# A graph attention layer on one core: x in four buffers, statistics spread over the step, and the masks made by GpSimd

## What is computed

```python
h = relu(layernorm(x))
q, k, v = h @ Wq + bq, h @ Wk + bk, h @ Wv + bv          # 12 heads
scores = q @ k.T / sqrt(32) + beta * adj
scores = where(adj > 0, scores, -9e15)
out = x + softmax(scores) @ v
```

## Time and profile before

| | us |
|---|---|
| median of 3 runs | 1084.06 (1083.67 to 1090.45) |
| the profiled execution | 1083.19 |
| span of its instructions | 1081.4 |
| TensorE busy | 995.7 (92%) |
| VectorE busy | 927.1 (86%) |
| ScalarE busy | 901.2 (83%) |
| GpSimd busy | 661.5 (61%) |
| TensorE's mean granted clock | 0.984 |

### The profile page before, as it was taken

One profiled execution on the slowest core, in us unless ns is written; L12 is line 12 of the kernel. 1 busy time (PEld: TensorE's weight loads), 2 busy tenths in 40 slices (PEclk: granted clock), 3 DMA queues, 4 the chain that ended last, 5 costly groups with the idle time before them and its releaser, 6 DMA issues.

```text
span 1081.4 us, 33411 instructions
## 1 busy us (share of the span) xinstructions
PE 995.7 (92%) x10587; PEld 674.7 (62%) x10587; DVE 927.1 (86%) x4256; ACT 901.2 (83%) x2384; POOL 661.5 (61%) x908
## 2 busy tenths in 40 slices
PE   3879999999999999999999999989999999999996
PEld 1346666666666666666666666656666666666764
DVE  6468889988888888888888888878888998889897
ACT  4368888888888888888888888878988889888887
POOL 2846666566765566755566766556766657676531
PEclk9889999999999999999999999998999999999997
DMA  4695688877669976767986757785678787868741
GB/s 155 112 184 103 160 158 177 182 141 134 157 152 167 173 153 133 160 147 170 168 174 137 148 155 162 172 177 114 141 162 167 172 176 142 146 143 163 149 105 45
DMA packets 234336, 163.15 MB, mean 151 GB/s; under 512 B 109744, under 2 KB 234160, under 8 KB 234160
## 3 DMA queue, kind: packets, MB, share of 16 engines
q1 hardware_dynamic: 233632, 160.23, 71.1%
q10 hardware_dynamic: 528, 0.79, 0.2%
HBM read 35.91 MB, written 25.17 MB: 56 GB/s over the span
## 4 chain that ended last, share of the span: by engine, by line
issue 22%; ACT 21%; POOL 20%; PE 16%; DVE 15%; DMA 2%; SPq 1%; POOLq 1%; DVEq 0%; ACTq 0%
ACT probs L541 11%; PE ps_p L463 9%; POOL v L358 7%; DVE biased L669 6%; POOL v L356 4%; PE ps_t L483 4%; ACT hn L556 4%; DVE kT L652 3%; POOL on L364 3%; DVE pT L675 3%; ACT qT L570 3%; POOL rstd L334 3%; ACT pT L575 2%; PE ps_s L475 2%; DMA xs<-in_x 2%
## 5 line engine op out<-in xcount | busy, mean ns | idle before, releaser
L541 ACT ACTIVATE probs<-biased,neg_max 128x128 f32<-128x128 f32 x1536 | 490.1, 395 | 95.2 <-DVE neg_max L669 85.0
L669 DVE CUSTOM_DVE_ANT_0 biased<-ps_s,mask 128x128 f32<-128x128 f32 x1536 | 354.2, 286 | 98.6 <-PE ps_s L475 61.7
L463 PE MATMUL ps_p<-hT,w 128*128 128x512 f16 x1728 | 420.7, 384 | 6.5 <-DVE qT L652 3.5
L364 POOL TENSOR_TENSOR on<-on,xb 128x384 f32<-128x384 f32 x128 | 127.5, 996 | 308.0 <-DVE on L690 308.0
L483 PE MATMUL ps_t<-ident,probs 128*128 128x128 f32 x1536 | 248.0, 284 | 33.7 <-ACT probs L541 26.2
L463 PEld LDWEIGHTS ps_p<-hT,w 128*128 128x128 f16 x1728 | 170.6, 99 | 160.5 <-issue 11.6
L675 DVE TENSOR_TENSOR pT<-ps_t,pT 128x512 f16<-128x512 f32 x384 | 263.5, 686 | 8.1 <-ACT pT L575 8.1
L575 ACT ACTIVATE pT<-ps_t 128x512 f16<-128x512 f32 x384 | 223.2, 581 | 1.0 <-PE ps_t L483 1.0
L463 PE MATMUL ps_p<-w,hT 128*128 128x384 f16 x1152 | 207.6, 326 | 0.0
L483 PEld LDWEIGHTS ps_t<-ident,probs 128*128 128x128 f32 x1536 | 162.6, 142 | 42.5 <-ACT probs L541 42.4
L475 PEld LDWEIGHTS ps_s<-k_st,q_st 96*128 96x128 f16 x1536 | 115.9, 98 | 97.2 <-DVE neg_max L669 20.8
(11 more groups left out here) (65 smaller groups left out, 1024.8 us busy)
## 6 DMA issues: line engine op xcount, KB each, us to landing
q_st<-qT SPq DMA_DIRECT2D x288, 128.0 KB, 3.3
k_st<-kT SPq DMA_DIRECT2D x288, 128.0 KB, 5.5
out<-on SPq DMA_DIRECT2D x128, 192.0 KB, 3.4
xs<-in_x SPq DMA_DIRECT2D x31, 768.0 KB, 6.1
adjs<-in_adj SPq DMA_DIRECT2D x32, 256.0 KB, 6.9
hT<-h_parts SPq DMA_TRANSPOSE x62, 4.4
xs<-in_x ACTq DMA_DIRECT2D x1, 768.0 KB, 6.3
k_st<-in_L_gnn_Wq SPq DMA_DIRECT2D x1, 576.0 KB, 6.5
```

What stands on the lines that cost most here:

```text
L364: pool.tensor_tensor(on[:, j % 2, :], on[:, j % 2, :], xb[:, par, j, :], ALU.add).then_inc(added, 1)
L463: mm = pe.matmul(dst, stationary, moving, start=m == 0, stop=m == MMS - 1)
L541: act.activation(probs[:, odd, i, :], biased[:, odd, i, :], ACT.Exp, bias=neg_max[:, odd, i:i + 1], scale=-1.0).then_inc(exp_done, 1)
L669: dve.tensor_tensor_reduce(out=biased[:, odd, i, :], in0=ps_s[:, i * N:(i + 1) * N], in1=mask[:, gp, v // CH, :], scale=-1.0, scalar=3.0e3 ...
```

## The change

There are four parts.

1. x has four buffers. x(1) and x(2) are loaded before the first step, and x(s+3) at the head of step s, behind the store of row block 1 and ahead of the first q spread; it waits for the readers of x(s-1).
2. The statistics of group s+2 are taken in step s one graph to a slot, in slots 0, 1, 9 and 10; `mean_var` has two buffers.
3. On GpSimd `rstd_of(s + 2)` stands in step s behind `split_v(s, ., 2)`, ahead of `add_x(s - 1, ., 1)`; before it was `rstd_of(s + 1)`, second in step s. `split_v(s, ., 2)` comes ahead of that addition too.
4. The mask is made by GpSimd, in three passes over 128x512 (two with one tensor input, one with two), behind `add_bias(s, ., 3)` and ahead of `add_x(s - 1, ., 0)`. VectorE's two passes are gone.

```diff
+    XB = 4
-        xs = sb("xs", [P, 2, G, D], F32)
+        xs = sb("xs", [P, XB, G, D], F32)
+        weighted = sb("weighted", [P, G, N], F32)
-        mean_var = sb("mean_var", [P, G, 2], F32)
+        mean_var = sb("mean_var", [P, 2, G, 2], F32)
...
-            sp.dma_start(xs[:, 1], x_v[1]).then_inc(x_in[1], 16)
+            for s in range(1, XB - 1):
+                sp.dma_start(xs[:, s], x_v[s]).then_inc(x_in[s], 16)
...
                 if 2 <= s <= STEPS:
                     store(s - 2, 1)
+                ahead = s + XB - 1
+                if ahead < STEPS:
+                    wait(sp, xb_done, G * s)
+                    wait(sp, normed, G * s)
+                    sp.nop(nofuse=True)
+                    sp.dma_start(xs[:, ahead % XB], x_v[ahead]).then_inc(x_in[ahead % XB], 16)
                 if proj:
                     spread(s, par, "q", 0)
...
-                if 0 <= s <= STEPS - 3:
-                    sp.wait_ge(xb_done, G * (s + 1))
-                    sp.wait_ge(normed, G * (s + 1))
-                    sp.nop(nofuse=True)
-                    sp.dma_start(xs[:, par], x_v[s + 2]).then_inc(x_in[par], 16)
...
+            def mask_of(s, par):
+                pool.wait_ge(adj_in, 16 * (s + 1))
+                wait(pool, biased_done, HPC * SLOTS * (s - 1))
+                pool.nop(nofuse=True)
+                wait(pool, mask_done, s)
+                pool.tensor_scalar(mask[:, par], adjs[:], 0.0, MASKED, ALU.is_le, ALU.mult).then_inc(mask_parts, 1)
+                pool.tensor_scalar(weighted[:], adjs[:], beta_col[:, 0:1], None, ALU.mult).then_inc(mask_parts, 1)
+                pool.wait_ge(mask_parts, 2 * (s + 1))
+                pool.tensor_tensor(mask[:, par], mask[:, par], weighted[:], ALU.add).then_inc(mask_done, 1)
...
                 if 1 <= s <= STEPS:
                     split_v(s - 1, 1 - par, G - 1)
-                if s >= 1 and s <= STEPS - 2:
-                    rstd_of(s + 1)
...
                 if proj:
                     add_bias(s, par, 3)
+                    mask_of(s, par)
                 if attend:
                     add_x(s - 1, 1 - par, 0)
                 if proj:
                     split_v(s, par, 0)
                     split_v(s, par, 1)
+                    split_v(s, par, 2)
+                if s <= STEPS - 3:
+                    rstd_of(s + 2, par)
                 if attend:
                     add_x(s - 1, 1 - par, 1)
-                if proj:
-                    split_v(s, par, 2)
...
-            def mask_unlinked(s, par):
-            def mask_linked(s, par):
...
+            def stats_in(s, u):
+                if s == 0:
+                    if u in (2, 3):
+                        return [(1, 2 * (u - 2)), (1, 2 * (u - 2) + 1)]
+                    return [(2, 2 * (u - 8)), (2, 2 * (u - 8) + 1)] if u in (8, 9) else []
+                at = {0: 0, 1: 1, 9: 2, 10: 3}
+                return [(s + 2, at[u])] if s <= STEPS - 3 and u in at else []
...
-                    if s <= STEPS - 3 and SLOTS - 2 <= u < SLOTS:
-                        for j in range(2 * (u - SLOTS + 2), 2 * (u - SLOTS + 3)):
-                            moments(s + 2, par, j)
+                    for t, j in stats_in(s, u):
+                        moments(t, j)
                     if ended:
                         scale_out(valued[1], valued[3] // CH)
-                    if proj and u == 4:
-                        mask_unlinked(s, par)
-                    if proj and u == 7:
-                        mask_linked(s, par)
...
+                    for t, j in stats_in(s, u):
+                        variance(t, t % 2, j)
```

More of the change, by code:

```diff
@@ L147, in graph_attention_kernel @@
         beta_in = sem("beta_in")
-        x_in = [sem(f"x_in{b}") for b in range(2)]
+        x_in = [sem(f"x_in{b}") for b in range(XB)]
         adj_in = sem("adj_in")
@@ L323, in _, with rstd_of @@
             pool.wait_ge(consts_set, 3)
-            def rstd_of(s):
+            def rstd_of(s, par):
                 wait(pool, var_done, G * (s + 1))
@@ L344, in split_tokens @@
                 pool.tensor_tensor(h_parts[:, j, 1], hn[:, j], h_parts[:, j, 0], ALU.subtract).then_inc(h_low, 1)
+            def mask_of(s, par):
[7 more added lines that the diff above has]
+                pool.tensor_tensor(mask[:, par], mask[:, par], weighted[:], ALU.add).then_inc(mask_done, 1)
             def add_bias(s, par, j):
-                wait(pool, x_in[par], 8 * (s - par) + 16)
+                pool.wait_ge(x_in[s % XB], 16 * (s // XB + 1))
                 wait(pool, added, G * (s - 2) + j + 1)
-                pool.tensor_tensor(xb[:, par, j, :], xs[:, par, j, :], bv_row[:], ALU.add).then_inc(xb_done, 1)
+                pool.tensor_tensor(xb[:, par, j, :], xs[:, s % XB, j, :], bv_row[:], ALU.add).then_inc(xb_done, 1)
             def split_v(s, par, j):
@@ L376, in step @@
                 if s == 0:
-                    rstd_of(1)
+                    rstd_of(1, 1)
                 if 0 <= s <= STEPS - 2:
@@ L403, in step @@
                     add_x(s - 1, 1 - par, 3)
-            rstd_of(0)
+            rstd_of(0, 0)
             w_c = w_raw[:, :, W_COLS[1]]
@@ L420, in _ @@
             pool.wait_ge(bv_in, 16)
+            pool.wait_ge(beta_in, 16)
             run_steps(step)
@@ L555, in normalise @@
                 wait(act, h_low, G * (s - 2) + j + 1)
-                act.activation(hn[:, j, :], xs[:, par, j, :], ACT.Relu, bias=shift[:, j:j + 1],
+                act.activation(hn[:, j, :], xs[:, s % XB, j, :], ACT.Relu, bias=shift[:, j:j + 1],
                                scale=rstd[:, j:j + 1]).then_inc(normed, 1)
@@ L616, in _, with moments, variance @@
         def _(dve):
-            def moments(s, par, j):
-                wait(dve, x_in[par], 8 * (s - par) + 16)
+            def moments(s, j):
+                dve.wait_ge(x_in[s % XB], 16 * (s // XB + 1))
                 wait(dve, var_done, G * (s - 1) + j + 1)
-                dve.bn_stats(stats[:, j, :], xs[:, par, j, :]).then_inc(stats_done, 1)
-            def variance(s, j):
-                wait(dve, rstd_done, s)
+                dve.bn_stats(stats[:, j, :], xs[:, s % XB, j, :]).then_inc(stats_done, 1)
+            def variance(s, par, j):
+                wait(dve, rstd_done, s - 1)
                 dve.wait_ge(stats_done, G * s + j + 1)
                 dve.nop(nofuse=True)
-                dve.bn_aggr(mean_var[:, j, :], stats[:, j, :]).then_inc(var_done, 1)
-            def mask_unlinked(s, par):
-                dve.wait_ge(adj_in, 16 * (s + 1))
-                wait(dve, biased_done, HPC * SLOTS * (s - 1))
-                dve.tensor_scalar(mask[:, par], adjs[:], 0.0, MASKED, ALU.is_le, ALU.mult).then_inc(unlinked, 1)
-            def mask_linked(s, par):
-                dve.wait_ge(unlinked, s + 1)
-                dve.scalar_tensor_tensor(out=mask[:, par], in0=adjs[:], scalar=beta_col[:, 0:1], in1=mask[:, par],
-                                         op0=ALU.mult, op1=ALU.add).then_inc(mask_done, 1)
+                dve.bn_aggr(mean_var[:, par, j, :], stats[:, j, :]).then_inc(var_done, 1)
             def first_low_part(bank, c):
@@ L706, in step @@
                         invert_sums(valued[1], valued[3] // CH)
[L707 to L712 removed]
+                    for t, j in stats_in(s, u):
+                        moments(t, j)
                     if ended:
                         scale_out(valued[1], valued[3] // CH)
[L715 to L724 removed]
+                    for t, j in stats_in(s, u):
+                        variance(t, t % 2, j)
             for j in range(G):
[L727 to L728 removed]
+                moments(0, j)
+                variance(0, 0, j)
             dve.wait_ge(b_in, 16 * 2)
@@ L793, in _ @@
             weights_low(2)
-            dve.wait_ge(beta_in, 16)
             dve.wait_ge(bias_set, 2)
```

17 lines of the change are left out of this document (3 added, 14 removed).

## The result

The changed kernel takes 1019.17 us (median of 4 runs, the fastest 1017.88), the kernel before 1085.36 beside it: ratio 0.938, 95% interval 0.934 to 0.942. One of the four took 5427.58 us, of which there is no trace; it counts in the median, while the ratio and its interval are of the other three (1017.88, 1018.47 and 1019.87). Forecast were 1020. Its profiled execution took 1018.47 us with a span of 1016.7, so 64.7 us of span are gone, where the sum had 64.4.

A forecast was written before the change was run, and what follows sets the result against it. No engine was full; TensorE waited 2.50 us of each 32.13 us step, mostly through late normalisations on ScalarE. Saving 62.4 us in 29 steps and 2 at the start takes 1084.06 to about 1020 us; range 1006 to 1050.

The forecast's parts named there:

- the sum: 29 steps going from 32.13 to 29.98 us give 62.4, the start 2: 64.4 us off the span.
- PE's own time of 29.63 us: Step 31, which normalises nothing, taken as a step in which TensorE never waits: 29.63 us against 32.13.
- The wait for x: VectorE's statistics wait for x, 0.7 us a step; gone with four buffers; PE feels part, inside 0.5 us a step.
- `rstd` early: On GpSimd ahead of the addition that waits for slot 11, it ends ScalarE's 1.48 us normalisation wait for `shift`.
- What is late next, ACT: ScalarE's exponentials come late after slots of 2.83 us; 0.35 us a step stays, giving a step of 29.98.
- C: `shift` stays late because GpSimd has more work; step 31.63, 1068 us; chance 0.09.
- E: The early load of x delays q spreads and transposes of h by as much as is gained; no change; chance 0.04.
- Rival B: ScalarE stays the bound in slots 3 to 5: 0.89 us stays, step 30.52, 1035 us; chance 0.22.
- The masks: Three GpSimd passes take 2.7 to 4.0 us a step, covered by idle time; cost 0, or 1 us at worst.
- signs of being right: Among others: scores 29.9 to 30.2 us apart, GpSimd busy 23 to 25 a step, mask passes 0.6 to 1.4 each.
- Rival D: GpSimd compares slowly and sets the step from 9.5 us of mask; at 15 us, 1183 us; chance 0.05.
- Start and tail: PE's 6.75 us idle before the first scores shrinks by 2 us, bounds 0 and 5; the tail keeps its time.

The follow-up runs named there:

- e10: Changed kernel with ScalarE's four normalisations of a step in slots 0, 1, 3 and 4 instead of 1, 2, 3 and 4: 1007.64 us, ratio 0.928.
- e1: Changed kernel with the masks made by VectorE again, in slots 4 and 7: 1022.54 us, ratio 0.941.
- e4: Kernel before with only x in four buffers, loaded at the head of the step: 1067.12 us, ratio 0.984.
- e2: Changed kernel with `rstd_of` alone moved back to its old place on GpSimd: 1018.86 us, ratio 0.938.
- e3: Changed kernel with the statistics back in slots 10 and 11, two in each: 1019.06 us, ratio 0.938.
- e2b: Changed kernel with `rstd_of` and the split of V block 2 both back behind GpSimd's addition of block 1: 1038.46 us, ratio 0.956.
- e8: Changed kernel with e2b's old GpSimd order and e3's statistics in slots 10 and 11 together: 1064.24 us, ratio 0.981.
- e5: Changed kernel with ScalarE's four normalisations in slots 0, 1, 2 and 4 instead of 1, 2, 3 and 4: 1010.16 us, ratio 0.932.
- e7: Changed kernel with three more passes, results unused, in GpSimd's mask: 1137.72 us (one run).
- e9: Changed kernel with one more pass, result unused, in GpSimd's mask: 1017.42 us, ratio 0.938.
- e11: e10 with SyncE's order in step 0 changed, k spreads ahead of transposes of h and adjacency last: 1005.49 us, ratio 0.927.
- e6: Changed kernel with GpSimd's first mask pass only comparing and its second multiplying by a constant 0.1: 1018.58 us (one run).

## Why the prediction was right

**PE's own time of 29.63 us: right but for 0.07.** e10 takes 29.58 with next to no wait left in its steps, and step 31 takes 29.56. In the kernel before, in e1 and in e4 it takes 29.63 or 29.64: the 0.07 is what the masks on VectorE cost in slot 10, in step 31 too, so 29.63 was not free of waiting.

**The wait for x: right, with one cause too many.** It is gone, and the 0.5 us a step with it (e4: 32.13 to 31.59). The prediction gave the 0.5 to x and the crowded slots together; e4 has the slots as crowded as before, so it was x. Its 0.7 us a step on VectorE was misread: of the 20.7 us left without the 9.8, another 7.0 lie at the start, which leaves 13.7 in 14 places, 0.47 us a step.

**`rstd` early: the wait goes, but the cause was named too narrowly.** The prediction had `rstd_of` standing behind two splits and the addition, and took its new place as the cure. The chain was rightly read, but more than the named link counts: the scaling in slot 11, the splits, `rstd_of`. e2 undoes the named link without a loss, e3 another without a loss, e2b, which undoes two, costs 0.65 us a step, and e8, which undoes all three, 1.60. What matters is how late the end of the chain is against the normalisation. Three edits of the change shorten it (the statistics out of slot 11, split 2 ahead of the addition, `rstd_of` ahead of it); without the first or without the last the rest is enough. The second alone was not undone.

**What is late next, ACT: right in place and size.** Forecast were exponentials 1.35, 1.66, 1.98 and 1.73 after their scores in slots 2 to 5; measured 1.49, 1.79, 2.08, 1.73. Forecast were 0.35 us left in slots 4 and 5; measured 0.09 + 0.31 = 0.40. Rival B, with 0.89 left, is thereby out, and e5 and e10 (9 and 11.5 us) show that it is ACT's queue.

**Rivals C and E: out.** C had `shift` late all the same. It is ready 1.9 us after a step's first scores and the normalisation comes at 5.7 (step 16 of the changed kernel). E had the early load of x delay the q spreads and the transposes of h by as much as is gained. e4 has that load and gains 17 us, and in steps 2 to 30 of the changed kernel PE waits for no transfer.

**The masks: cost 0 right for the time, the term itself wrong.** 4.80 us a step, not 2.7 and not the upper bound of 4.0; GpSimd's 25.2 us a step and two of its three passes lie outside what the prediction named as signs of being right (23 to 25, and 0.6 to 1.4 each). The two-input pass came as scaled (1.33 forecast, 1.27 measured). The step that failed is the pricing of the one-input passes by the cast, 0.67 each; they took 1.95 and 1.58. The idle time covered them all the same, but the margin was thin: 1.3 us at the copy of v block 2, not the 3.9 of idle time that the prediction set against the upper bound. By e1 taking the masks off VectorE gave back about 0.1 us a step, which the prediction had at nothing.

**Rival D: right not to happen, its price wrong.** It took GpSimd's busy time as the limit: GpSimd would set the step from 9.5 us of mask, and the kernel be slower than before from 11.6. e7 has 9.45 us of mask and takes 1137.72, 5% more than before. The limit is the split of v behind the mask, and e9, at 6.4 us, stands at it.

**Start and tail: small terms, both off.** 2 us forecast at the start, 0.8 measured: the first scores wait for the last k spreads, which go out after the adjacency as before (53.40 now, 53.49 then), so the earlier x loads left them alone; e11 moves them and gains the 2. The tail gave 1.0 us where 0 was forecast; no run looked into why. Neither figure is sure: in the runs that keep this start (e7 left out) the time ahead of step 2 is 82.7 to 85.6, and the tail, 35.0 before and 34.0 now, is 34.0 to 34.8 in all experiments but e7 (35.5); each was profiled once. The two errors cancel, which is luck. The 62.8 for 62.4 in the steps is not, since its terms hold one by one; that it is so close is luck in part, as 29.56 + 0.40 stands for 29.63 + 0.35.

## What to carry over

A late value has a chain behind it, and its wait is the difference between the time at which the value is ready and the time at which it is needed. Once enough links have been shortened, a further one gives nothing; undoing one edit alone may then show no cost, while undoing two or three together brings the wait back (here 0, 0.65 and 1.60 us a step). So test such edits together too, and not only one by one. Room on an engine is not its idle share but the slack of the next thing in its queue that somebody waits for; read it as the distance between that operation's end and its reader's start. Where one engine lags, compare its work slot by slot with the pace of the engine that it feeds, and move work out of runs of full slots: other slots for four normalisations were worth 11 us here.

## What the runs showed of the hardware

On GpSimd an operation of a tensor with a scalar took longer here than an addition of two tensors. 512 float32 columns take 1.27 us as an addition of two tensors, but 1.50 us as one operation with a scalar, 1.58 with the scalar from SBUF, and 1.95 with two operations (e6 and the changed kernel). The casts of 384 columns, at 0.503 to 0.506 us the only other wide passes with one input, do not give their price. The first mask pass, a comparison and a multiplication, is the same instruction that VectorE had: 0.417 us there when GpSimd is not in its way, 1.95 on GpSimd. The Trainium skill, "GPSIMD Engine Reference", section 4.1, says that one-input work on GpSimd is roughly at line rate, and two-input work about twice as slow as on VectorE. The first does not fit these rows, where one input takes longer than two and 4.7 times as long as on VectorE; the second is tested by no run here.

How long VectorE's old mask pass took, from 417 to 1172 ns, went with the GpSimd instruction that was under way. VectorE and GpSimd of the kernel before, at two of its 32 places:

```profile
98.96 0.68 DVE L632 TENSOR_SCALAR mask<-adjs 128x512 f32<-128x512 f32 x1
```

```profile
98.86 0.50 POOL L342 CAST h_parts<-hn 128x384 f16<-128x384 f32 x1 [0.37 <-ACT hn L556]
```

```profile
67.29 1.17 DVE L632 TENSOR_SCALAR mask<-adjs 128x512 f32<-128x512 f32 x1
```

```profile
67.27 0.92 POOL L344 TENSOR_TENSOR h_parts<-hn,h_parts 128x384 f16<-128x384 f32 x1
```

The pass ends 0.28 us after the cast ends (99.64, 99.36) and 0.27 after the subtraction ends (68.46, 68.19), as if it did its work only once GpSimd was through. At 26 of the 32 places the cast is under way as in the first, and the pass takes 673 to 681 ns; at five none is when the pass begins, or for at most 0.14 us more, and it takes 417 to 419. The other way round GpSimd's subtraction beside a mask pass was stretched: it took 971 to 980 ns in 27 places and 1237 in one, and now never over 923. Least, median and greatest ns of that line, before and after:

```profile
L344 POOL TENSOR_TENSOR h_parts<-hn,h_parts x124: 909/917/1237, 39.4 to 1001.7; 128x384 f16<-128x384 f32 x124
```

```profile
L350 POOL TENSOR_TENSOR h_parts<-hn,h_parts x124: 909/917/923, 40.6 to 938.2; 128x384 f16<-128x384 f32 x124
```

This agrees with the Trainium skill, "SBUF — State Buffer", section "Who interferes with whom", by which whoever issues first holds the shared port pair for its whole instruction. The price was small here: some 0.26 us a step on VectorE and 0.06 on GpSimd.
